# Graph layers on one core: logits tiles between two parts of a propagation unit, and three reorderings on ScalarE and VectorE

## The reference, cut to what matters

```python
h = jnp.maximum(_layernorm(x, axis=-1), 0.0)
x = x + L1(h, adj)

def L1(X, S):                                   # N = 2048, d = 128
    R = S + eye(N);  R = R / R.sum(-1, keepdims=True)
    Z = 0;  Xf = X;  Xa = X
    for n in range(2):                          # two steps
        q = Xa @ W1.T @ W2.T;  k = Xa @ W3.T
        probs = softmax(q @ k.T)                # N x N
        A = probs with only the largest entries of a row kept,
            until their sum reaches 0.9; rows scaled back to 1
        Xf = R @ Xf
        Xa = A @ Xa
        Z = Z + Xf @ U1[n].T + Xa @ U2[n].T
    return layernorm(X + Z) * ln_g + ln_b
```

## Time and profile before

| | |
|---|---|
| median of 3 runs | 1072.84 us (1069.78 to 1074.75) |
| the profiled execution | 1073.61 us, its span 1071.8 us |
| busy: PE, DVE, ACT, POOL | 838.4, 779.4, 509.2, 70.5 us |
| step 0 and step 1 of the second layer | about 139 to 505 us, and 505 to 850 us |

### The profile page before, as it was taken

How to read it: one execution, slowest core, us unless ns; L and a number is a source line. 1 busy time by engine, 2 the same in 40 slices (tenths; PEclk the granted TensorE clock), 3 DMA queues, 4 the chain that set the end, 5 groups by cost and what they waited for, 6 DMA issues and landing times.

```text
span 1071.8 us, 12286 instructions
## 1 busy us (share of the span) xinstructions
PE 838.4 (78%) x3886; PEld 563.7 (53%) x3886; DVE 779.4 (73%) x2363; ACT 509.2 (48%) x979; POOL 70.5 (7%) x68
## 2 busy tenths in 40 slices
PE   4879958887887843839778978868289899996795
PEld 4844325555655633737356557547258475553342
DVE  5978679888998998961797889789799502326715
ACT  4877235357367376314452664764765332023212
POOL 0020110000000000000000000010000200002201
PEclk9999987888988985969799789979689999998798
DMA  9949203334004000000044220220152546500001
GB/s 335 354 173 430 104 29 129 130 106 158 1 1 158 1 1 1 1 2 1 1 157 149 87 79 1 94 119 1 49 209 78 230 161 245 226 1 0 1 0 39
DMA packets 20221, 108.25 MB, mean 101 GB/s; under 512 B 1824, under 2 KB 8752, under 8 KB 9776
## 3 DMA queue, kind: packets, MB, share of 16 engines
q1 hardware_dynamic: 18752, 106.77, 26.7%
q10 hardware_dynamic: 1392, 0.61, 0.2%
HBM read 88.23 MB, written 19.14 MB: 100 GB/s over the span
## 4 chain that ended last, share of the span: by engine, by line
PE 47%; DVE 29%; ACT 11%; issue 9%; POOL 2%; DMA 1%; DVEq 1%; POOLq 0%; SPq 0%; ACTq 0%
DVE AT L1525 9%; PE PS L808 9%; PE PS L743 7%; PE PS L676 5%; PE PS L880 5%; PE PS L546 4%; DVE mxv L1664 4%; DVE nd L1528 3%; PE PS L1063 3%; PE PS L1039 3%; DVE AT L2111 2%; PE PS L1069 2%; ACT BC L1252 2%; ACT AT L1252 2%; ACT AT L1085 1%
## 5 line engine op out<-in xcount | busy, mean ns | idle before, releaser
L1085 ACT ACTIVATE AT<-PS 128x512 f32<-128x512 f32 (+2 forms) x240 | 118.2, 562 | 127.1 <-PE PS L546 107.8
L743 PE MATMUL PS<-K,ST 128*128 128x512 f32 x224 | 129.4, 731 | 15.7 <-ACT EA L1220 8.1
L546 PE MATMUL PS<-ident,AT 128*128 128x128 f32 x544 | 84.1, 289 | 42.5 <-DVE AT L1525 18.0
L1525 DVE SCALAR_TENSOR_TENSOR AT<-EA,se 128x2048 uint8<-128x2048 f32 (+1 forms) x46 | 107.6, 2345 | 1.6 <-DVE se L1518 0.3
L1525 DVE SCALAR_TENSOR_TENSOR AT<-AT 128x2048 uint8<-128x2048 f32 (+2 forms) x48 | 96.1, 2002 | 1.8 <-PE PS L546 0.8
L1664 DVE TENSOR_REDUCE mxv<-PS 128x1 f32<-128x2048 f32 x32 | 73.3, 2289 | 30.4 <-PE PS L743 24.7
L546 PEld LDWEIGHTS PS<-ident,AT 128*128 128x128 f32 x544 | 67.5, 150 | 50.9 <-DVE AT L1525 18.9
L743 PEld LDWEIGHTS PS<-K,ST 128*128 128x128 f32 x224 | 50.6, 238 | 78.1 <-issue 78.0
L2111 DVE MAX8 AT<-AT 128x8 f32<-128x256 f32 x256 | 87.6, 411 | 0.7
L808 PE MATMUL PS<-hr,AT 128*128 128x128 f32 x512 | 69.2, 284 | 8.5 <-ACT AT L1085 7.7
L808 PE MATMUL PS<-AT 128*128 128x128 f32 x512 | 67.4, 279 | 10.2 <-ACT AT L1085 9.7
(11 more groups left out here) (297 smaller groups left out, 1471.1 us busy)
## 6 DMA issues: line engine op xcount, KB each, us to landing
AT<-keep_at SPq DMA_DIRECT2D x32, 1024.0 KB, 5.1
EA<-in_adj SPq DMA_DIRECT2D x20, 1024.0 KB, 6.8
keep_at<-AT SPq DMA_DIRECT2D x8, 2048.0 KB, 24.9
AT<-keep_at SPq DMA_DIRECT2D x8, 2048.0 KB, 12.2
AT<-in_adj SPq DMA_DIRECT2D x12, 1024.0 KB, 5.7
EA<-keep_degrees SPq DMA_DIRECT2D x1, 1024.0 KB, 6.4
keep_x<-K SPq DMA_DIRECT2D x4, 256.0 KB, 8.6
out<-EA SPq DMA_DIRECT2D x4, 256.0 KB, 2.3
```

The costliest lines, as they stand in the source:

```text
L546: return pe.transpose(dst, src, ident[0:p, 0:p])
L743: mm = pe.matmul(bank(half(gi, k) + n), ST[1][:, k * P:(k + 1) * P], wide_keys[:, n * BK:(n + 1) * BK], start=True, stop=True)
L1085: return act.activation(dst, src, ACT.Copy)
L1525: return dve.scalar_tensor_tensor(out=o, in0=x0, scalar=s, in1=x1, op0=op0, op1=op1, **k)
```

## The change

Four pieces, all of them of order.

1. In group 0 of each step TensorE doesn't do logits tile, whole unit, logits tile, whole unit any more. The third logits tile goes ahead of the second unit's turns and products, and the fourth between the two halves of the third unit. ScalarE does the third and fourth exponential ahead of the third unit's copies, and the last unit comes behind the guess.
2. On ScalarE the exponential of the second tile goes behind the fourth copy of an attend tile (`b == 3` instead of 2), and the guess ahead of the former tile's result (`result_out`) instead of behind it.
3. In the third sum of the groups that aren't first, the next group's second row maximum goes behind the second tile's pass instead of the first's.
4. Where a group follows, the doubt flags are computed after the next group's last tile, their instructions alternating with those of the surplus (`doubtful_with_sums`); so they no longer stand ahead of that pass, and eight of them stand behind the wait for ScalarE's sums.

No instruction is added or removed among those that compute.

```diff
--- before.py
+++ after.py
@@ -596,23 +596,22 @@
                     tr = turn(bank(6)[:, k * P:(k + 1) * P], ST[q][:, k * P:(k + 1) * P])
                 tr.then_inc(ps_t, 1)
 
-            def unit_sums(u):
-
-
-                p, c = u // UNITS, u % UNITS
+            def unit_freed(u):
+
                 if u == UNITS:
                     pe.wait_ge(un_row, UNITS)
                 if u > 0:
                     pe.wait_ge(un_st, u)
                     pe.wait_ge(un_row, min(u, UNITS))
+
+            def unit_part(u, h):
+
+                p, c = u // UNITS, u % UNITS
                 left = hr if p == 0 else Xf
-                for j in range(NT):
-                    if j % HALF == 0:
-                        pe.wait_ge(slab_in[j // HALF], 16 * (u + 1))
+                pe.wait_ge(slab_in[h], 16 * (u + 1))
+                for j in range(h * HALF, (h + 1) * HALF):
                     mm = pe.matmul(bank(6)[:, 2 * P:4 * P], left[:, j, :], slab[:, j, :],
                                    start=(j == 0), stop=(j == NT - 1))
-                    if j == HALF - 1:
-                        mm.then_inc(un_half, 1)
                     if j == 0:
                         for k in range(2):
                             pe.matmul(bank(6)[:, (2 + k) * P:(3 + k) * P], left[:, 2 * c + k, :], ident[:, :],
@@ -745,12 +744,18 @@
                                    start=True, stop=True)
                 mm.then_inc(logits_ok, 1)
 
-            def unit(step, g, u, early=False):
+            def unit_begun(step, g, u, early=False):
 
                 pe.wait_ge(mean_ok, NB * step + (2 if early else min(g + 3, NB)))
                 if step + g > 0:
                     pe.wait_ge(z_ok, G * (NB * step + g))
-                unit_sums(u)
+                unit_freed(u)
+                unit_part(u, 0)
+
+            def unit(step, g, u, early=False):
+
+                unit_begun(step, g, u, early)
+                unit_part(u, 1)
                 unit_rows(u)
 
             def result_turned(step, g, k):
@@ -933,10 +938,20 @@
                             attend(step, g - 1, k, (lambda: logits(step, g + 1, k + 1)) if more and k < G - 1 else None,
                                    g - 2 if step == 1 and g > 1 else None)
                         else:
+                            at = units_by(NB * step) + k
                             if k > 0:
                                 logits(step, 1, k)
-                            if k < UNITS_IN[NB * step]:
-                                unit(step, 0, units_by(NB * step) + k, True)
+                            if k == 2:
+                                unit_rows(at - 1)
+                            if k == 3:
+                                unit_part(at - 1, 1)
+                                unit_rows(at - 1)
+                            if k == 1 or k == 2:
+                                unit_begun(step, 0, at, True)
+                            if k == 1:
+                                unit_part(at, 1)
+                            if k == 0 or k == 3:
+                                unit(step, 0, at, True)
                     if g < NB - 2:
                         queries(step, g + 2)
                         means(step, g + 2)
@@ -1280,11 +1295,11 @@
                     if u > 1:
                         act.wait_ge(ex_mm, u - 1)
                     copy(stg[b % 2], bank(4 + b % 2)).then_inc(e_copied, 1)
+                    if b == 1 and between:
+                        between()
                     if b == 1 and k > 0:
                         result_out(k - 1)
-                    if b == 1 and between:
-                        between()
-                    if b == 2 and inside:
+                    if b == 3 and inside:
                         inside()
                 act.wait_ge(ex_mm, 4 * c + 4)
                 dst = xa_rows[:, G * g + k, :] if step == 0 else T[:, k, :]
@@ -1402,8 +1417,9 @@
                             exponential(step, 1, k)
                         if g > 0 and more and 0 < k < G - 1:
                             exponential(step, g + 1, k + 1)
-                        if g == 0:
+                        if g == 0 and k != 2:
                             if k == G - 1:
+                                unit_next()
                                 guess(step, 1)
                             unit_next()
                     if g < NB - 2:
@@ -1928,11 +1944,11 @@
                 q = guess_of[gi % 2]
                 mass_above(E, gi, 0)
                 remember(q, 1)
-                if gi not in BOTH:
-                    between()
                 mass_above(E, gi, 1)
                 v.wait(1)
                 weigh(q)
+                if gi not in BOTH:
+                    between()
                 mass_above(E, gi, 2)
                 v.wait(1)
                 weighed()
@@ -2070,6 +2086,36 @@
                 v(tt(s_(4), s_(4), s_(3), ALU.max))
                 v(dve.tensor_reduce(fl[:, 0:1], s_(4), AX.X, ALU.max))
                 any_row(v)
+
+            def doubtful_with_sums(nq, n):
+
+
+                mass_above(EA if n % 2 == 0 else EB, n, G - 1)
+                v.wait(1)
+                v.put(tt(s_(3), s_(3), s_(4), ALU.max))
+                v.put(tt(fl[:, TIE:TIE + G], after, s_(0), ALU.is_ge))
+                v.put(tt(s_(5), seen8, s_(0), ALU.is_ge))
+                v.wait(2)
+                v.put(tt(s_(4), after, s_(0), ALU.is_ge))
+                v.wait(1)
+                v.put(tt(s_(3), s_(5), s_(3), ALU.max))
+                dve.wait_ge(sum_ok, sums_by(n, 0) + 2 * (G - 1))
+                v.put(stt(pa, below[:, 1, :], float(N), ALU.add, nq.th, ALU.mult))
+                v.wait(1)
+                v.put(dve.tensor_reduce(fl[:, UNSURE:UNSURE + 1], s_(3), AX.X, ALU.max))
+                v.put(tt(s_(4), s_(4), s_(3), ALU.max))
+                v.put(tt(pb, below[:, 0, :], nq.spare, ALU.add))
+                v.wait(1)
+                v.put(dve.tensor_reduce(fl[:, 0:1], s_(4), AX.X, ALU.max))
+                v.wait(1)
+                v.put(stt(nq.fval, pa, -0.5, ALU.mult, pb, ALU.add))
+                v.wait(1)
+                v.put(dve.transpose(ft[:, :], fl[:, :]))
+                v.wait(1)
+                v.put(tt(nq.fval[:, G - 1:G], Fv[:, G - 1:G], nq.Tt[:, G - 1:G], ALU.subtract))
+                v.wait(1)
+                v.put(dve.tensor_reduce(fl[:, 1:2], ft[:, :], AX.X, ALU.max))
+                v.wait(1)
 
             def group(E, gi, left):
 
@@ -2127,11 +2173,10 @@
                 if left > 1:
                     logit_mean(gi + 2)
                 crossing_checked(q)
-                doubtful()
-                if left > 0:
-                    last_tile(nq, gi + 1)
-                    surplus_below(nq, gi + 1, 0)
-                    last_surplus(nq)
+                if left == 0:
+                    doubtful()
+                else:
+                    doubtful_with_sums(nq, gi + 1)
                     first_step(nq)
                     dve.sem_inc(th_ok, 1)
                     remember(nq, 0)
```

## The result

The changed kernel takes 1074.43 us (median of 20 runs, 1073.02 to 1077.53) against 1072.70 us before (20 runs, 1069.07 to 1075.13): ratio 1.002, 95% interval 1.0012 to 1.0029. It is 0.2% slower, inside the 0.5% called "no change", but the other way than the forecast's 1070.1. The profiled execution took 1077.36 us, 2.9 above the kernel's own median; that of before was 0.9 above its own. So the two executions lie 3.8 us apart where the medians lie 1.7 apart: they show where time goes, not the total to a microsecond.

A forecast was written before the change was run, and what follows sets the result against it. Hand-overs between TensorE, VectorE and ScalarE, none always busy, were taken as the bound. Group shifts ran from -0.65 after step 0's group 0 to -2.7 after step 1's group 2, taking 1072.84 to 1070.1 us; range 1064 to 1076.

The forecast's parts named there:

- The guess ahead of the result's copy: ScalarE's guess delays TensorE's projection by 1.23 us, less 0.10: +1.13 us, paid in three of four groups.
- rival d: TensorE's break before first groups' last unit halves its clock: first part +1.7 a step, 1073.5, chance 0.12; whole unit 1085, 0.08.
- rival a: The guess's new place on ScalarE is free because the gap comes early: 1066.7 us, chance 0.20.
- rival (c): Waits between small instructions cost nothing, so interleaving the doubt flags saves nothing: 1074.7 us, chance 0.05.
- The last unit of the first groups: After a TensorE break of about 1.8 us it ends at 225.5, yet queries and sums move by only -0.06.
- The forecast's own signs of being wrong: Sums' start moving over 1 us, last unit at half clock, or logits tiles changing speed where nothing was moved.
- The late sums: VectorE, earlier everywhere, waits for ScalarE's sums in all six groups, some 5 us in first groups; each late sum costs +0.21.
- The doubt flags: VectorE's new instruction order saves 1.13 us in each of six groups if the sums are there, +0.21 if late.
- The second maximum: Moved behind another VectorE pass, +2.35 in step 0's group 1; with ScalarE's earlier copy, +0.50, -1.46, -1.61, -1.90 by group.
- Step 1's group 2: TensorE has other rows to sum, its turns hold VectorE's next pass anyway: guess counted +0.26 and -0.26.

The follow-up runs named there:

- after_guess_last: The changed kernel with the guess put back behind the result's copies, the other three edits kept: 1067.78 us, ratio 0.9954.
- d_only: The kernel before with only the doubt flags mixed with the next group's sums: 1071.25 us, ratio 0.9984.
- m_only: The kernel before with only the next group's second maximum and its exponential moved: 1072.12 us, ratio 1.0000.
- m_and_d: The kernel before with the second maximum and the doubt flags moved, units and guess as before: 1067.70 us, ratio 0.9958.
- after_fill: The changed kernel with four matmuls on nothing needed ahead of the last projection of groups 0 and 1 of each step: 1079.53 us, ratio 1.0054.
- g_fill: The kernel before with only the guess moved ahead, plus four matmuls on nothing needed ahead of the late projection: 1079.97 us, ratio 1.0068.

## Why the prediction was wrong

**The guess ahead of the result's copy** is the step that failed in size. It was priced at 1.13 us in three groups, 3.4 in all; it measured 2.9, 3.5 and 3.0 us in the trace and 6.7 in the medians, against a kernel whose old place isn't free either (1.65, 1.67 and 0.03 us in after_guess_last's trace). The wait was about right (TensorE idle 1.04 us; 1.33 us in all at full clock, with the fill). Missing was the term for half clock, put at nothing here, which takes 1.65 us and more where VectorE hangs on every turn, and which all six unfilled guesses had. The forecast did weigh a clock drop after a break, but only for the units (rival d). With the guess out, the forecast would have been 1066.7 (its rival a) and the kernel measures 1067.8: the remaining edits together come out within 1.1 us. 3.3 of the 4.3 us of error are the guess's. The good sum of the rest is partly luck, for its terms were off both ways: the last unit by +2.0 us in step 0 and the second maximum by what is said below. Nor is the shift passed on by every stage behind step 1's group 2: it falls from +4.9 at that group's first step to +3.3 at the end. Luck, too, is that rival (c)'s 1074.7 lies next to the measured 1074.43: d_only went the other way than it says.

**The last unit of the first groups**: rival (d), first part, is what happened in step 0, and not in step 1, where the unit stayed quick. It named +1.7 us a step; in step 0 the unit took 9.3 instead of 7.5, and the first step of group 0 came at +1.37 and not at -0.65. The forecast's own signs of being wrong, sums that start over 1 us later and a unit (here a part of it) at half clock, both came. The reason given against it, quick matmuls behind a break of 1.87 us at 226.01, was one instance and a row of 0.44 us; the changed kernel has the same quick row behind its break (217.47), and is slow only from 218.83 on. Yet this didn't decide the total: with units and guess undone the kernel takes 1067.70, with the units alone put back 1067.78. Their 5 us on VectorE turn into a wait for the sums, as forecast.

**The late sums**: right. The wait is 4.79 us where some 5 were named, and from its end to the first step it is 0.87 us (245.95 to 246.82), as laid out from the distances of 0.08 and 0.20. All six sums came late, by 0.48 to 4.79 us of waiting, as counted. Of the eight instructions behind the wait's own, five are of the flags (ten in all, not eleven) and three of the surplus. The doubt flags alone give 1.4 us. Rival (c) is out.

**The second maximum**: +2.35 in group 1 came as +2.36, and it shows no wait for TensorE later. Its total alone (-0.6) was far from the -4.5 that the group terms (+0.50, -1.46, -1.61, -1.90) sum to; with the doubt flags 3.3 remain for it. m_only's trace says where: its group 1 comes out 2.0 us later and not 0.5, with the third tile at 5.30 us, and step 1's group 1 +0.2 and not -1.6, with half clock at the last pass (1.67 of the table above), while step 0's group 2 has -1.7. From 172.85 us on its profiled execution gains 4.1 us, its median only 0.6; why was not tested.

**Step 1's group 2**: the guess's early place took VectorE's wait of 4.64 us away, and its last pass then waited 3.06 us for TensorE's turns, as forecast. That this pass still comes 1.83 us earlier, measured from the fourth maximum, is hardly the guess's: it is 1.63 with the guess in its old place in m_only, m_and_d and after_guess_last, whose clock stayed up there, while the kernel before had half clock from 748.9 to 752.3.

## What to carry to other kernels

A wait put ahead of TensorE, even one of 1 us, is to be priced twice: with the matmuls behind it at the rate of the quick rows and at that of the slow ones, on every chain that hangs on them. Before a break is blamed for slow matmuls, look whether the clock fell before or behind it, and in more than one trace. Before ScalarE is given something else ahead of a copy that TensorE waits for, ask what TensorE has meanwhile; if nothing, leave the copy first. A microsecond won on TensorE ahead of a hand-over that another engine fixes can merely lengthen the break there, and come back as a slow tile.

## What was not expected of the hardware

The same break doesn't always have the same end. In step 1's group 2 the changed kernel and after_fill ran the same instructions up to a break of 2.15 us; behind it the first eight instructions took 1.16 us in one trace and 1.57 in the other, and the pairs of the row sums 0.39 and 0.65:

```profile
755.43 1.16 PE L813 MATMUL PS<-AT 128*128 128x128 f32 x8 [2.15 <-ACT AT L1100]
```

```profile
755.41 1.57 PE L813 MATMUL PS<-AT 128*128 128x128 f32 x8 [2.15 <-ACT AT L1103]
756.77 0.65 PE L875 MATMUL PS<-WT,ST 128*128 128x128 f32 x2
```

The fill of after_fill came only behind these rows. And filling a break doesn't buy the clock for good: it was 1.00 in group 1 of g_fill and 0.68 in its group 2. Runs of one kernel without any edit scatter by 6 us (1069.07 to 1075.13), and the traces of these kernels differ by up to 3.1 us already at 172.85, ahead of every edit; how much of that is the clock was not measured.
